# Probabilities that come back in two transfers, and values in quarters: an attention kernel on one NeuronCore

## What is computed

```python
k = jnp.einsum('ihd,bpd->biph', W_K, x)
q = jnp.einsum('ihd,bpd->biph', W_Q, x)
v = jnp.einsum('ihd,bpd->biph', W_V, x)
scores = jnp.einsum('biph,biqh->biqp', k, q)
masked = scores * mask - jnp.float32(10000000000.0) * (1.0 - mask)
attn = jax.nn.softmax(masked / jnp.sqrt(jnp.float32(d_head)), axis=-1)
z = jnp.einsum('biqp,biph->biqh', attn, v)
out = jnp.einsum('df,bqf->bqd', W_O, z_flat)
...
x = x + _L0_attn_ref(xn, ...) + _L0_ffn_ref(xn, ...)
```

## Time and profile before

| what | value |
|---|---|
| median of 3 runs | 1411.65 us |
| profiled execution | 1413.05 us, of which the span from first to last instruction is 1411.0 us |
| granted TensorE clock, mean | 0.984 |
| busy: PE, DVE, ACT, POOL | 1342.5, 938.8, 950.2, 961.2 us |
| DMA | 330.72 MB in 275741 packets, 74.6% of 16 engines over the span |

### The profile page before, as it was taken

One profiled execution on the slowest core, in us unless ns is written; L12 is line 12 of the kernel. 1 busy time (PEld: TensorE's weight loads), 2 busy tenths in 40 slices (PEclk: granted clock), 3 DMA queues, 4 the chain that ended last, 5 costly groups with the idle time before them and its releaser, 6 DMA issues.

```text
span 1411.0 us, 26546 instructions
## 1 busy us (share of the span) xinstructions
PE 1342.5 (95%) x8138; PEld 1198.1 (85%) x8138; DVE 938.8 (67%) x2131; ACT 950.2 (67%) x1926; POOL 961.2 (68%) x634
## 2 busy tenths in 40 slices
PE   6999999999999999999999999999999999999987
PEld 5788888788888888888888888888888888888876
DVE  6544200767767777777777777787777777777763
ACT  4332344677768777778776877787778777877774
POOL 6111000277869787879787978797879787978794
PEclk9999999999999999999999999999999999999999
DMA  4200166797888889888888898888898889898883
GB/s 151 71 1 0 37 193 189 205 293 252 263 271 258 287 259 288 259 285 259 281 258 270 272 283 269 286 266 287 259 286 264 287 262 290 256 287 263 278 252 98
DMA packets 275741, 330.72 MB, mean 234 GB/s; under 512 B 62576, under 2 KB 248048, under 8 KB 271344
## 3 DMA queue, kind: packets, MB, share of 16 engines
q1 hardware_dynamic: 275696, 330.19, 74.6%
HBM read 170.85 MB, written 159.25 MB: 234 GB/s over the span
## 4 chain that ended last, share of the span: by engine, by line
POOL 41%; issue 29%; PE 17%; DMA 4%; SPq 3%; DVE 3%; ACT 2%; POOLq 1%; ACTq 0%; DVEq 0%
POOL pt_lo L462 28%; POOL acc L453 9%; PE ps L970 6%; PE ps L971 6%; PE ps L972 6%; SPq L353 3%; DMA scratch<-raw 3%; POOL v_lo L467 3%; DMA pt_lo<-scratch 1%; POOL wqk_lo L442 1%; DVE raw L902 1%; ACT raw L655 1%; POOLq L461 1%; DVE had L892 0%; DVE pt_lo L913 0%
## 5 line engine op out<-in xcount | busy, mean ns | idle before, releaser
L462 POOL TENSOR_TENSOR pt_lo<-pt_lo,pt_hi 128x896 fp32r<-128x896 f32 (+2 forms) x378 | 651.8, 1756 | 140.1 <-ACT pt_hi L662 140.0
L655 ACT ACTIVATE raw<-ps,had 128x1024 f32<-128x1024 f32 (+7 forms) x384 | 329.4, 867 | 163.6 <-DVE had L895 133.7
L902 DVE STREAM_TRANSPOSE raw<-raw 128x2048 f32<-128x2048 f32 (+3 forms) x252 | 317.0, 1292 | 105.5 <-ACT raw L655 103.2
L970 PE MATMUL ps<-pt_hi,v_hi 128*128 128x256 f32 (+1 forms) x1152 | 327.1, 284 | 35.1 <-POOL v_lo L467 27.4
L971 PE MATMUL ps<-pt_lo,v_hi 128*128 128x256 f32 (+1 forms) x1152 | 333.2, 289 | 0.0
L972 PE MATMUL ps<-pt_hi,v_lo 128*128 128x256 f32 (+1 forms) x1152 | 331.0, 287 | 0.0
L662 ACT CAST pt_hi<-pt_lo 128x896 fp32r<-128x896 f32 (+2 forms) x378 | 284.5, 818 | 35.4 <-DMA pt_lo<-scratch 35.1
L892 DVE TENSOR_REDUCE had<-ps 128x1 f32<-128x1024 f32 (+1 forms) x256 | 237.4, 947 | 46.9 <-PE ps L972 46.7
L970 PEld LDWEIGHTS ps<-pt_hi,v_hi 128*128 128x128 f32 x1152 | 223.2, 194 | 46.0 <-POOL v_lo L467 30.6
L970 PE MATMUL ps<-k_hi,q_hi 128*128 128x512 f32 (+3 forms) x640 | 235.7, 368 | 7.0 <-DVE k_lo L866 5.9
L971 PE MATMUL ps<-k_lo,q_hi 128*128 128x512 f32 (+3 forms) x640 | 233.8, 365 | 0.0
(11 more groups left out here) (113 smaller groups left out, 2222.6 us busy)
## 6 DMA issues: line engine op xcount, KB each, us to landing
v_next<-all_values SPq DMA_DIRECT2D x16, 1024.0 KB, 5.4
scratch<-raw SPq DMA_DIRECT2D x64, 256.0 KB, 5.6
pt_lo<-scratch SPq DMA_DIRECT2D x16, 1024.0 KB, 5.4
scratch<-raw SPq DMA_DIRECT2D x64, 240.0 KB, 5.0
pt_lo<-scratch SPq DMA_DIRECT2D x16, 960.0 KB, 5.9
scratch<-raw SPq DMA_DIRECT2D x64, 224.0 KB, 5.2
pt_lo<-scratch SPq DMA_DIRECT2D x16, 896.0 KB, 4.7
scratch<-raw SPq DMA_DIRECT2D x64, 208.0 KB, 4.7
```

The costliest lines, as they stand in the source:

```text
L462: pool.tensor_tensor(lo, lo.bitcast(F32), hi.bitcast(F32), ALU.subtract).then_inc(pt_lo_done, 1)
L655: act.activation(to, scores, ACT.Exp, bias=neg_max[:, j:j + 1], accum_out=row_part[:, j, e % 2:e % 2 + 1]).then_inc(exped, 1)
L902: dve.transpose(v, v).then_inc(blocked, 1)
L970: pe.matmul(dst, a[0], b[0], start=start, stop=False, skip_group_check=True)
```

## The change

The big row's bring becomes two transfers, one for each piece of key tiles, with a semaphore each, so that `p_to_hi` of the first piece no longer waits for the whole row. Both the first and the second half now have four runs per partition. The values come in quarters: 3 and 2 after the sends of step 6, 0 after those of step 7, 1 after those of the next head's step 0. Quarters 0 and 1 are split at the beginning of step 4: on ACT ahead of the exponentials, on POOL ahead of an `add`. On ACT, the copy of K's quarter 2 moves ahead of the probabilities in step 7, and in the last head the order at the end differs.

```diff
@@ -90,6 +90,8 @@
 
     V_ITEMS = [3, 2, 0, 1]
     V_AT = {0: [3], 3: [2], 4: [0, 1]}
+
+    V_NEXT = {6: (3, 2), 7: (0,)}
     KQ_FIRST = 6
 
     with ExitStack() as ctx:
@@ -241,13 +243,13 @@
         qk_split, wo_split = sem("qk_split"), sem("wo_split")
         projected, proj_hi, proj_lo = sem("projected"), sem("proj_hi"), sem("proj_lo")
         v_projected, v_copied, v_stored = sem("v_projected"), sem("v_copied"), [sem("v_stored0"), sem("v_stored1")]
-        v_moved = sem("v_moved")
+        v_moved = [sem(f"v_moved{b}") for b in range(QUARTERS)]
         late_projected, late_copied = sem("late_projected"), sem("late_copied")
         late_stored = [sem(f"late_stored{i}") for i in range(4)]
         v_hi_done, v_lo_done, v2_read = sem("v_hi_done"), sem("v_lo_done"), sem("v2_read")
         scored, maxed, negmaxed, exped = sem("scored"), sem("maxed"), sem("negmaxed"), sem("exped")
         blocked = sem("blocked")
-        stored, moved = [sem("stored_big"), sem("stored_small")], [sem("moved_big"), sem("moved_small")]
+        stored, moved = [sem("stored_big"), sem("stored_small")], [sem("moved_big0"), sem("moved_big1"), sem("moved_small")]
         pt_hi_done, pt_lo_done = sem("pt_hi_done"), sem("pt_lo_done")
         transposed, t_hi_done, t_lo_done = sem("transposed"), sem("t_hi_done"), sem("t_lo_done")
         z_product, z_hi_done, z_lo_done = sem("z_product"), sem("z_hi_done"), sem("z_lo_done")
@@ -361,19 +363,25 @@
 
                     wait(sp, z_product, (z_count(h - 1, 5), z_count(h - 1, 7),
                                          z_count(h, 1 if small else 0), z_count(h, 3 if small else 2))[m])
-                wait(sp, moved[small], 16 * (STEPS * h + s))
                 sp.wait_ge(stored[small], 64 * (STEPS * h + s + 1))
-                to = pt_row(pt_lo, j).bitcast(F32).rearrange("p a i q -> p a (i q)")
-                sp.dma_start(to, scratch[j].rearrange("p (a x) -> p a x", a=4)).then_inc(moved[small], 16)
-
-            def bring_v(h):
-
-                wait(sp, v_lo_done, QUARTERS * h)
-                sp.dma_start(v_next[:, :], all_values[h].rearrange("p i d -> p (i d)")).then_inc(v_moved, 16)
+                back = scratch[j].rearrange("p (a i q) -> p a i q", a=4, q=BLK)
+                for n in (2,) if small else (0, 1):
+                    first, last = piece_keys(j, n)
+                    wait(sp, moved[n], 16 * (STEPS * h + s))
+                    sp.dma_start(pt_row(pt_lo, j, first, last).bitcast(F32).rearrange("p a i q -> p a (i q)"),
+                                 back[:, :, first:last, :].rearrange("p a i q -> p a (i q)")).then_inc(moved[n], 16)
+
+            def bring_v(h, b):
+
+                wait(sp, v_lo_done, v_count(h - 1, b))
+                sp.dma_start(v_next[:, b * BANK:(b + 1) * BANK],
+                             all_values[h][:, b * PER_Q:(b + 1) * PER_Q, :].rearrange("p i d -> p (i d)")
+                             ).then_inc(v_moved[b], 16)
 
             for i in range(2):
                 sp.wait_ge(v_stored[i], 16 * TILES // 2)
-            bring_v(0)
+            for b in V_ITEMS:
+                bring_v(0, b)
             for h in range(HEADS):
                 for s in range(STEPS):
                     if s == 0 and h + 1 < HEADS:
@@ -395,8 +403,10 @@
                     if h == 0 and s == 5:
                         for i in range(4):
                             sp.wait_ge(late_stored[i], 16 * LATE_UNITS // 4)
-                    if s == 5 and h + 1 < HEADS:
-                        bring_v(h + 1)
+                    for b in V_NEXT.get(s, ()) if h + 1 < HEADS else ():
+                        bring_v(h + 1, b)
+                    if s == 0 and h > 0:
+                        bring_v(h, V_ITEMS[-1])
             for z in range(CHUNKS):
                 c = Z_ORDER[z]
                 sp.wait_ge(out_added, z_count(HEADS - 1, z))
@@ -470,6 +480,8 @@
             def period(h, first=False, more=True, over=False):
 
                 for s in range(5 if over else STEPS):
+                    for b in V_AT[4] if s == 4 and not over else []:
+                        v_to_lo(h, b)
                     if (s - 1) in O_BIG or s == 0:
                         back, z = O_BIG[(s - 1) % STEPS]
                         if s == 0:
@@ -478,7 +490,7 @@
                             add(h + back, z)
                     if s == 2 and more and not over:
                         split_qk(h + 1)
-                    for b in [] if over else V_AT.get(s, []):
+                    for b in [] if over or s == 4 else V_AT.get(s, []):
                         v_to_lo(h, b)
                     if s == 4 and not over:
                         split_o(h)
@@ -624,7 +636,7 @@
 
             def v_to_hi(h, b):
                 sl = slice(b * BANK, (b + 1) * BANK)
-                act.wait_ge(v_moved, 16 * h + 16)
+                act.wait_ge(v_moved[b], 16 * h + 16)
 
                 if b == 3:
                     wait(act, z_product, z_count(h - 1, 2))
@@ -658,7 +670,7 @@
             def p_to_hi(h, s, n):
                 j = row_of(s, n == 2)
                 a, b = piece_keys(j, n)
-                act.wait_ge(moved[n == 2], 16 * (STEPS * h + s + 1))
+                act.wait_ge(moved[n], 16 * (STEPS * h + s + 1))
                 act.copy(pt_row(pt_hi, j, a, b), pt_row(pt_lo, j, a, b).bitcast(F32)).then_inc(pt_hi_done, 1)
 
             def transposed_to_hi(n):
@@ -688,7 +700,7 @@
                     return first and back or over and not back
 
                 for s in range(5 if over else STEPS):
-                    if s == 0 and not absent(O_SMALL[s][0]):
+                    if s == 0 and not absent(O_SMALL[s][0]) and not over:
                         z_to_hi(h + O_SMALL[s][0], O_SMALL[s][1])
                     if (s - 1) in O_BIG or s == 0:
                         back, z = O_BIG[(s - 1) % STEPS]
@@ -696,8 +708,8 @@
                             back -= 1
                         if not absent(back):
                             output(h + back, z)
-                    if s == 3 and not over:
-                        v_to_hi(h, 2)
+                    for b in V_AT[s] if s in (3, 4) and not over else []:
+                        v_to_hi(h, b)
                     if s in (1, 3) and not absent(O_BIG[s][0]):
                         z_to_hi(h + O_BIG[s][0], O_BIG[s][1])
                     if not over:
@@ -724,9 +736,10 @@
                     if s == 3 and more and not over:
                         kq_to_hi(h, ("K", 3))
                     if s >= 5 and more and not over:
-                        kq_to_hi(h, (("Q", 3), ("Q", 0), ("K", 1))[s - 5])
-                    for b in [] if over or s == 3 else V_AT.get(s, []):
-                        v_to_hi(h, b)
+                        for item in ([("Q", 3)], [("Q", 0)], [("K", 1), ("K", 2)])[s - 5]:
+                            kq_to_hi(h, item)
+                    if s == 0 and not over:
+                        v_to_hi(h, V_ITEMS[0])
                     if first and s < 4:
                         late_copy(2 * s)
                         late_copy(2 * s + 1)
@@ -734,16 +747,15 @@
                     if over and s < 2:
                         for n in range(5):
                             transposed_to_hi(5 * s + n)
-                    if not (first and s < 2) and not over:
+                    if not (first and s < 2) and not over and not (s == 7 and not more):
                         p_to_hi(hh, ss, 0)
-                    if s in (1, 3, 5) and not absent(Z_SMALL[s][0]):
+                    if s in ((1, 3, 5) if more else Z_SMALL) and not absent(Z_SMALL[s][0]):
                         z_to_hi(h + Z_SMALL[s][0], Z_SMALL[s][1])
                     if not (first and s < 2) and not over:
+                        if s == 7 and not more:
+                            p_to_hi(hh, ss, 0)
                         p_to_hi(hh, ss, 1)
                         p_to_hi(hh, ss, 2)
-                    if s == 7 and more:
-                        kq_to_hi(h, ("K", 2))
-
             act.activation(table_use[:, 2:3], ones[:, :], ACT.Exp)
             qk_to_hi(0)
             for i, n in V_UNITS:
```

## The result

The changed kernel took 1438.68 us (median of 4 runs, 1437.77 to 1442.83) where the kernel before took 1409.65 on the same chip: a ratio of 1.0217 estimated over the runs of both, 95% interval 1.0188 to 1.0247 (the two medians alone give 1.0206). It is slower, by 29.0 us between the medians, in the forecast's direction and range and 12 us under its 1451. The profiled execution took 1439.23 us with a span of 1437.2.

What follows compares the result with a forecast made beforehand. The prediction took SP's ring of transfers as the bound: 61.4 us for runs and starts less 22.5 us for the value load, 38.9 us more, gave 1451 us, slower by 2.8%, range 1388 to 1475.

Steps and rivals of the forecast that it cites:

- SP's ring of stores and returns: SP's queue: wait for stores, bring, send, wait again; claimed to set the pace, with the engines not late.
- Runs and starts: Big-row returns: shorter runs and starting with many runs cost 3.9 us a head, 61.4 us in 15.75 heads.
- the smaller runs: Big-row returns in runs of 1 KB to 512 B move slower: 1.5 us a head, 0.3 of it even rows.
- the starts: Returns starting with many runs: 0.59 us for each of four rows that had one run, 2.4 us a head.
- The value load in quarters: Value load on SP: quarters fit a step's 1.2 us idle time, saving 1.5 us in 15 heads, 22.5 us.
- The rival of SP's issues: SP's queue: eight more brings and three more loads cost 6.3 us a head, 99 us, giving 1488 us; chance 0.10.
- the held sends: SP's eight sends are held by a full queue, 2.8 us a step, so one more issue costs nothing.
- The sum: Over the whole kernel: 61.4 us of cost less 22.5 us from the value load, 38.9 us more.
- The value split at step 4: On POOL and ACT: low values ready 1.8 us sooner, but worth nothing because PE then waits for the pieces.
- What was to show it: Signs: SP steps of 8.7 to 9.2 us, none of 10 with value load, DMA share over 0.87, more packets.
- The faster one: Big-row returns: small runs cost nothing, only the value load counts, 1389 us, floor 1384; chance 0.24.
- that of cancelling effects: Starts hide in the pause; runs cost 23.6 us and the load gives 22.5 back: 1413 us; chance 0.13.

Runs made afterwards that it cites:

- SP's order alone: SP issues bring big, send big, bring small, send small, instead of both brings then both sends: kernel before 1392.95 us; changed kernel 1403.75 us.
- the split alone: The kernel before with the big row's return in two transfers by key tiles, nothing else of the change: 1447.18 us, 1.0266.
- The even rows: The kernel before with the split by key tiles only for rows 14, 12, 10 and 8, odd rows whole: 1406.91 us, 0.9978.
- the halves: The kernel before with the big row's return in two transfers, each of two of its four 32-query blocks for all key tiles: 1391.75 us, 0.9850.
- four transfers: The kernel before with the big row split by key tiles and each piece in two transfers of two of its four blocks: 1479.03 us, 1.0495.
- the kernel with four quarters at step 5: The kernel before with the value load in four transfers of 256 KB, all at the old place after step 5's sends: 1425.10 us, 1.0106.
- The kernel with the best time: The kernel before with SP's bring-send order by row, big returns by halves of blocks, the change's ACT and POOL order, whole value load: 1375.52 us, 0.9761.

## Why the prediction was right, and where it was not

**What bounds the kernel** held. SP's ring of stores and returns sets the pace: SP's order alone gives 17 us before and 35 us after the change, and the earlier value split, which takes most of PE's largest wait away, gives 3.7.

**Runs and starts** have the right sign, and the odd rows are the right place, but the term was mis-sized: 61.4 us forecast, 37.6 measured alone. For the split alone, the smaller runs were put at 1.5 us a head, and the DMA was busy 1.5 longer; the starts were put at 2.4, and the idle part grew by 1.5, both from the profiled execution, whose heads show more than the 2.4 us a head of the medians. In the changed kernel as a whole the busy part grew by 3.1 and the idle part fell, so this division is a reading and not shown. The 0.59 us of a start came from one pair of steps; over 13 heads the same pair, rows 12 and 11, differs by 0.29. Nor are the starts shared out evenly: 0.59 was put on each of four odd rows, where the table has 1.33, 0.74, 0.08 and 0.35. The part of the smaller runs that I gave to the even rows was free. By the rule of the Trainium skill, page "DMA: Bandwidth & Descriptors", section "Specifications", transfers of 512 B and more are at line rate. The even rows agree with it, taken as a rule on runs (ratio 0.9978); that the DMA is busy 1.5 us a head longer for the same bytes in the split alone does not.

**The value load in quarters** failed, in the step "two quarters nearly fit and one fits. I let the whole 1.5 us go". The 1.5 us did go (1.71), but each quarter is an issue and a transfer in a ring without room for it. Alone they cost 6.6 us where -22.5 was forecast. The rival of SP's issues had this price, 0.44 us for a load; I had let the held sends cover it for all issues. A second bring is covered (in the halves and in the even rows it costs nothing that shows), but not by the sends, whose time stays near 45 us a head (45.9 before): SP waits less for stores instead. Loads that stand behind the sends and ahead of a bring that did not wait are not covered.

**The sum** came so near partly by luck. Its two errors have opposite signs and nearly cancel: the parts measured alone, +37.6, +6.6 and -3.7, make 40.5 where 38.9 was forecast. Together they cost 29.0, and this, with a median of the kernel before that is now 2 us lower, is why 1451 was 12 us too high: the parts do not add. A reason would be that what one part leaves idle another uses; that is not shown. In the company of the rest the split is worth 1.0217 against 1.0012, 29 us, and the quarters and the order together nothing.

**The value split at step 4** was put at nothing and gave 3.7 us alone. In the changed kernel PE does wait elsewhere instead, but for `z_lo` (29.4) and `aux` (12.1), and not, as I had said, for `pt_lo` from POOL (1.1).

**What was to show it**, point by point: of the odd rows' steps one (8.94) lies in 8.7 to 9.2, the others are 9.65, 8.28 and 10.09, two of them with quarters; a 10 us step remains, with two quarters; the DMA share rose to 0.89 while GB/s fell from 273 to 266, right; 6199 packets a head more, right; ACT's wait for `pt_lo<-scratch` rose from 26 to 68 times, right in kind, but its larger new wait is for `raw`.

**The rivals.** The faster one fell with the split alone (+2.66%), that of cancelling effects with the quarters, which have nothing to give. That of SP's issues counted every added issue in full, 99 us. The issues did grow, to 61.4 us of SP's 72.45 a head from 54.6 of 70.55, but the DMA share rose with them, and brings added in the even rows or as halves cost nothing that shows. It holds for the loads, and is open for four transfers.

## What to carry to other kernels

When one queue waits for its stores, returns them and only then sends on, look for the order in which some independent transfer stands ahead of each wait: that was worth 17 us here, as much as the better choice of the transfers' sizes, and 35 in the kernel with the short runs. Split a transfer along the dimension that leaves its runs long (18 us faster here) and not along the one that cuts them (38 us slower), and count small loads in such a queue by their issues. A large wait on the busiest engine is no proof that the engine sets the pace: taking most of a 27 us wait away gave 4 us.

## What the runs showed of the hardware

Two transfers of 256 runs begin to move sooner than one of 512: a share of 0.78 against 0.55 in the second microsecond of row 14's step, and 8.11 against 8.62 us a step. The key split in four transfers of 256 runs costs 69 us, which neither the start nor the runs' number (equal in the split with two) explains.

The clock of TensorE fell after the pause at the values in some heads. In the kernel with four quarters at step 5 PE's timeline shows the pause, and windows of one microsecond the clock after it:

```profile
655.06 0.39 PE L974 MATMUL ps<-pt_hi,v_hi 128*128 128x256 f32 x1 [2.16 <-POOL v_lo L471]
```

```profile
654.26:655.26 1.00, 0.20 (x1) 0.20 (x2) 0.28 (x3) 0.88 (x3) 1.00 (x2) 1.00 0.22 45
655.26:656.26 1.00, 1.00 (x7) 1.00 (x7) 0.00 (x0) 1.00 (x2) 1.00 (x2) 0.60 0.45 80
656.26:657.26 1.00, 1.00 (x6) 1.00 (x6) 0.00 (x0) 0.10 (x2) 1.00 (x1) 0.50 1.08 278
657.26:658.26 1.00, 1.00 (x6) 1.00 (x6) 0.00 (x0) 0.00 (x0) 1.00 (x2) 0.50 1.01 332
```

PE had done nothing for 2.16 us; from 655.26 it ran for some three microseconds at about the lower level (0.50, 1.2 GHz). It does not follow each time: in the kernel before PE paused for 2.3 us from 723.4, and the granted clock stayed at 1.00. The kernel with the best time keeps 1.00 throughout its eleven heads. This is not the change's slowdown, since the changed kernel has 1.00 too. In the kernel with four quarters at step 5 it may be part of the loss, which was not tried apart: its eleven heads are 11 us longer than before, and PE is busy some 7 us longer in them.
